# Fewer FFN tiles a pair, scores from a product of the query and key weights, and half-array matmuls in a fused tokenizer, attention and FFN kernel

## The reference

```python
loc  = dwconv(gelu(conv(x, pl_w, stride=16)))          # depthwise 3x3, then 192x192
glob = conv(gelu(dwconv(gelu(conv(wavelet_packet(x), pg_w1)))), pg_w2)
h = (1 - gate) * loc + gate * glob
h = relu(dwconv(h, f1)); h = relu(dwconv(h, f2)); h = dwconv(loc + h, f3)
h = concat([cls, layernorm(h), txt])                    # 1 + 196 + 128 = 325 rows
# attention, each of q, k, v = gelu(x @ w1 + b1) @ w2 + b2 on x = layernorm(h)
scores = (q @ k.T) / SCALE * mask                       # 0 <= i - j < 64, no softmax
h = h + layernorm(scores @ v) * ln_w + ln_b
# FFN: two linear layers, activations rounded to 8 bits a row, weights to -1, 0, 1
h = h + bitlinear(silu(gate) * up, w_out), [up, gate] = bitlinear(layernorm(h), w_in)
```

## Time and profile before

| | us |
|---|---|
| median of the runs | 1199.82 |
| span of the profiled execution | 1195.4 |
| PE busy | 1081.3 (90%) |
| DVE busy | 1033.5 (86%) |
| ACT busy | 963.3 (81%) |
| POOL busy | 812.7 (68%) |

### The profile page before, as it was taken

The page is one execution under the profiler, slowest core; times in us unless marked ns, Lnnn a source line. Parts: engine busy times, 40 slices in busy tenths (PEclk is TensorE's granted clock), DMA queues, the critical chain, the costliest instruction groups (busy, mean ns, idle before and its releaser), DMA issues.

```text
span 1195.4 us, 19559 instructions
## 1 busy us (share of the span) xinstructions
PE 1081.3 (90%) x5674; PEld 736.5 (62%) x5674; DVE 1033.5 (86%) x3013; ACT 963.3 (81%) x2437; POOL 812.7 (68%) x860
## 2 busy tenths in 40 slices
PE   6877999999999999999999999999999897878544
PEld 3655676767676767677676757676766655545311
DVE  1887598999999999999999999999999997856653
ACT  4656687899989898989999988989898978766543
POOL 4446486868687777878686868787786857562521
PEclk9898999999999999999999999999999998979655
DMA  8101010101010100101010101001010000000000
GB/s 327 62 27 41 8 41 7 50 7 57 9 57 9 46 17 16 49 13 50 13 53 7 56 9 54 9 16 50 16 47 15 10 11 15 10 15 9 9 12 14
DMA packets 21513, 40.25 MB, mean 34 GB/s; under 512 B 2656, under 2 KB 18208, under 8 KB 19104
## 3 DMA queue, kind: packets, MB, share of 16 engines
q1 hardware_dynamic: 21408, 39.01, 9.4%
HBM read 31.02 MB, written 7.99 MB: 33 GB/s over the span
## 4 chain that ended last, share of the span: by engine, by line
PE 76%; DVE 9%; ACT 7%; issue 4%; POOL 2%; DMA 1%; SPq 0%; POOLq 0%; DVEq 0%; ACTq 0%
PE bank L398 14%; PE bank L517 7%; PE bank L428 7%; PE bank L439 4%; PE bank L430 4%; PE bank L438 4%; PE bank L376 4%; PE bank L377 3%; PE bank L539 3%; PE bank L458 3%; PE bank L459 3%; DVE bank L1214 2%; PE bank L471 2%; PE bank L472 2%; PE bank L587 2%
## 5 line engine op out<-in xcount | busy, mean ns | idle before, releaser
L1214 DVE SCALAR_TENSOR_TENSOR bank<-padA,c_col,bank 128x406 f32<-128x406 f32 x560 | 357.9, 639 | 7.6
L398 PE MATMUL bank<-x_sb,w_emb 128*128 128x392 f32 x576 | 216.6, 507 | 6.5 <-ACT padA L755 3.7
L810 ACT ACTIVATE prod<-padB,c_col 128x196 f32<-128x196 f32 x432 | 174.3, 449 | 5.1 <-POOL accB L1734 2.5
L1703 POOL TENSOR_TENSOR yg<-y_f,c_gout 128x512 f32<-128x512 f32 (+1 forms) x96 | 122.6, 1278 | 45.9 <-DVE y_f L1404 45.8
L398 PEld LDWEIGHTS bank<-x_sb,w_emb 128*128 128x128 f32 x576 | 102.3, 192 | 60.8 <-ACT padA L755 5.6
L810 ACT ACTIVATE early<-padB,c_col 128x196 f32<-128x196 f32 x288 | 120.7, 449 | 2.3 <-POOL accB L1734 2.2
L517 PE MATMUL bank<-w_in,xq 128*128 128x512 bf16 (+1 forms) x384 | 109.1, 411 | 13.6 <-ACT xq L873 13.6
L1696 POOL TENSOR_TENSOR s<-s,c_mhalf 128x1 f32<-128x1 f32 (+1 forms) x96 | 55.2, 575 | 90.8 <-ACT s L886 90.8
L867 ACT ACTIVATE yq<-bank 128x512 bf16<-128x512 f16 (+1 forms) x96 | 50.2, 523 | 50.8 <-PE bank L529 50.8
L879 ACT ACTIVATE th<-bank,sm 128x512 f32<-128x512 f32 (+1 forms) x96 | 65.3, 681 | 31.6 <-PE bank L517 31.1
L1385 DVE SCALAR_TENSOR_TENSOR ya<-th,bank 128x512 f32<-128x512 f32 (+1 forms) x96 | 65.1, 678 | 26.5 <-ACT th L879 26.3
(11 more groups left out here) (219 smaller groups left out, 3229.3 us busy)
## 6 DMA issues: line engine op xcount, KB each, us to landing
x_sb<-xt SPq DMA_DIRECT2D x16, 1176.0 KB, 5.3
out<-o_sb SPq DMA_DIRECT2D x64, 96.0 KB
w_sq<-squares SPq DMA_DIRECT2D x1, 3840.0 KB, 15.6
h_sb<-txt SPq DMA_DIRECT2D x32, 51.8 KB
out<-o_sb SPq DMA_DIRECT2D x32, 51.8 KB
h_sb<-txt SPq DMA_DIRECT2D x32, 44.2 KB
w_in<-win SPq DMA_DIRECT2D x1, 1024.0 KB, 17.6
c_row<-broads SPq DMA_DIRECT2D x1, 672.0 KB, 19.2
```

The lines of the kernel that those rows point to most:

```text
L398: done = mm(pE[:, 0:2 * N_PATCH], w_emb[:, k, m, :], x_sb[:, k, :], start=k == 0, stop=k == KC - 1)
L810: made = go(grid(prod[ACC[s] ^ 1][:, k, :]), tap_view(padB[min(s, 2)], SIDE, k), ACT.Copy, scale=tapcol(s, 1, k))
L1214: v.scalar_tensor_tensor(grid(acc if k == TAPS - 1 else run), tap_view(pad, ROWS_A, k), tapcol(s, 0, k), grid(run), ALU.mult, ALU.add).the ...
L1703: g.tensor_tensor(yg[0:m, :], y_f[0:m, :], c_gout[0:m, :], ALU.mult).then_inc(f_yg, 1)
```

## The change

Four things are done at once, and the order of every engine's turn is written anew.

1. **Five full FFN tiles a pair.** Rows 256 to 319 of both images make one tile of 128 rows. The last 5 rows of each image are gathered over many pairs in `left`, and worked on as a sixth tile in pairs 11 (120 rows) and 15 (40 rows). There are 82 tiles for 96. `join` on SP copies rows by three transfers inside SBUF: two into `left`, and, after these have landed, one of 64 rows that puts image 1 beside image 0.
2. **Scores from the product of query and key weights.** Once, the kernel computes the product of `qw2` and `kw2` and puts it in the place of `kw2`. The query's second layer and its four evictions on ACT go; scores are taken between the new keys and `hq`. What the query bias contributes for each key row is a vector, nine matmuls of one or two columns a pair, which DVE reads (`key_offsets`) and adds in `scores_out`.
3. **Tiles for half-used matmuls.** The first two matmuls of a square's third chunk become column tiles; the last matmuls of `values` (the two full row tiles), `scores` and `layer_F3` become pairs of row tiles, one for each image.
4. **Order.** All turns are reordered, with 8 stages and 23 turns; PE's first stage with work is now `on[1]`, its last `on[7]`. `values` and `scores` of both images are interleaved.

```diff
             def square(i, chunks, dstA, dstB, n, after):
...
-                mm(dstB, w[:, AB0, :], chunks[0], start=True, stop=False)
-                mm(dstB, w[:, AB1, :], chunks[1], start=False, stop=False)
+                for c in range(2):
+                    mm(dstB[HALF[c]], w[:, AB0 + c, HALF[c]], chunks[c], start=True, stop=False)
                 mm(dstB, w[:, BB, :], chunks[2], start=False, stop=True).then_inc(after, 1)
...
+            def scores(a):
+                took(a, U_K2 + 2)
+                unit_free(a, U_SC)
+                for t in range(TILES):
+                    r = pT[U_SC % 2][0:ROWS[t], R_AT + 2 * t:R_AT + 2 * t + 2]
+                    mm(r, hk[:, 2, tok_cols(t)], c_qk[:, 0:2], start=True, stop=False)
+                    for img in range(2):
+                        mm(r[:, img:img + 1], hk[:, img, tok_cols(t)], c_qk[:, 2:3], start=False, stop=img == 1)
+                unit_free(a, U_SC + 1)
...
-                    mm(dst, k2[:, img, tok_cols(t)], q2[:, img, q], start=True, stop=False)
-                    done = mm(dst, k2[:, 2, tok_cols(t)], q2[:, 2 + img, q], start=False, stop=True)
+                    for img in range(2):
+                        mm(dst[img], k2[:, img, tok_cols(t)], hq[:, img, q], start=True, stop=False)
+                    for img in range(2):
+                        done = mm(dst[img], k2[HALF[img], 2, tok_cols(t)], hq[HALF[img], 2, q], start=False, stop=True)
...
+            def query_key_weights():
+                pe.wait_ge(s_cst, ALL_CONSTS)
...
+                done.then_inc(s_qk, 1)
+                pe.wait_ge(s_qkw, 2)
+                for half in range(2):
+                    for o in range(2):
+                        mm(pT[0][:, half * D:(half + 1) * D], t_k2[cut[o], o, half * P:(half + 1) * P],
+                           t_q2[cut[o], o, 0:D], start=o == 0, stop=o == 1)
...
+            def join(f, par):
+                sp.wait_ge(h2_ready, f + 1)
+                lo = left_rows(f) - 2 * SPARE
+                for img in range(2):
+                    sp.dma_start(left[f > LEFT[0]][lo + img * SPARE:lo + (img + 1) * SPARE, :],
+                                 h2[par][SPAN:ROWS[2], 2 + img * TILES, :]).then_inc(taken, 16)
+                sp.wait_ge(taken, (f + 1) * 32)
+                sp.dma_start(h2[par][SPAN:P, 2, :], h2[par][0:SPAN, 2 + TILES, :]).then_inc(joined, 16)
...
                 for n in tiles:
-                    m = ROWS[n % TILES]
-                    done = v.bn_stats(st_f[0:m, n, :], h2[par][0:m, n, :])
+                    if n == 2:
+                        dve.wait_ge(joined, (f + 1) * 16)
+                    done = v.bn_stats(st_f[:, n, :], h2[par][:, n, :])
...
+            def query_key_blocks():
...
+                dve.wait_ge(s_qk, 1)
+                for t, bank_ in ((t_q2, pT[0]), (t_k2, pT[1])):
...
+                dve.wait_ge(s_qk, 2)
+                w, top, low = w_sq[:, SQUARES.index("kw2")], HALF[0], HALF[1]
+                v.tensor_copy(w[:, AA, :], pT[0][:, 0:P])
...
             def turn(it, par, on):
...
+                if on[5]:
+                    hidden_bn(it - 5, odd, (0, 1, 3))
+                if on[6]:
+                    hidden_round(3, it - 6, 3, par)
+                if on[2]:
+                    taps(it - 2, L_, 6)
+                if on[6]:
+                    hidden_round(4, it - 6, 3, par)
+                    gated(it - 6, 4)
+                if on[2]:
+                    taps(it - 2, L_, 7)
+                if on[6]:
+                    lifted(it - 6, 4)
+                if on[5]:
+                    hidden_bn(it - 5, odd, (4, 2))
```

The last store of a pair with leftover rows is one transfer for each image, 24 for pair 11 and 8 for pair 15:

```diff
+                if n == NF:
+                    for i in range(left_rows(f) // SPARE):
+                        image = 2 * f + 2 - left_rows(f) // SPARE + i
+                        sp.dma_start(out[image, T - SPARE:T, :],
+                                     o_sb[at][i * SPARE:(i + 1) * SPARE, :]).then_inc(stored[at], 16)
```

## The result

The changed kernel takes 1271.24 us (median of 4 runs, 1269.59 to 1274.97) where the one before, beside it, takes 1199.81: a ratio of 1.0604, 95% interval 1.0577 to 1.0631. Slower by 71 us; 1164 was predicted, with a range that ends at 1193.

What follows compares the result with a forecast made beforehand. The prediction took PE to bound the middle of the kernel. From the profiled 1195.4 us, 30 saved in steady turns, 12 saved in the drain and 6 lost in the fill, plus 4.4 to the median, gave 1164 us, range 1132 to 1193.

Steps and rivals of the forecast that it cites:

- its own sign: Stated test: the prediction is wrong if PE rests more than 2 us a turn or the key vector costs over 3.
- PE's sum: PE's work in a middle turn: 3.38 + 1.03 - 1.5 - 0.5 = 2.4 us saved, a turn of 62.5 us.
- the terms 0.01 and 0.04: Tiles on PE: each of five squares gains 0.01 us a turn, each of six row pairs loses 0.04.
- Both stay hidden, and PE is their cover: Middle turns: DVE falls to 60.6 us, 1.9 behind PE, ACT loses work, so neither sets the turn.
- Rival C: The new order leaves holes in PE: 1179 us if half the gain goes, 1194 if all; chance 0.18.
- The steady 30 us: Middle of the kernel: 12.5 turns at 2.4 us each save 30 us (0 to 51).
- so a turn of 62.5 us: Middle: PE's work after the saving of 2.4 us was taken as the length of the turn.
- The fill: Start of the kernel: making the product of the weights in the third turn loses 6 us (0 to 10).
- PE's second step: Fill: PE's multiplication of the query and key weights, after its transposes, put at 3 us.
- The drain: End of the kernel: fewer FFN tiles save 14 us, eight stores cost 2.3, net 12 us saved.
- where the last attention is the limit: Drain: lower bound of 5 us for the tiles' saving, if the last attention limits instead of the FFN tiles.
- Rival D: Slower by the join: two transfer hops of 4.5 us each make DVE wait, 24 us slower, 1224; chance 0.10.

Runs made afterwards that it cites:

- e1: Changed kernel with POOL's sums for layer F3 held back until DVE's `token_scale_3` is through; 1222.8 us, 1.0205 of the kernel before.
- e9: Changed kernel: F3 sums wait, `biased_tokens` later, two EMB_GA chunks earlier, weight product over two turns, SP's stores of tiles 2 and 3 before text loads; 1201.3 us.
- e5: Kernel before with only the column pairs in the five squares and F3's row pairs added; 1201.8 us, 1.0017 of the kernel before.
- e2: Changed kernel with two EMB_GA chunks on PE moved ahead of the pair's first token transposes; 1240.0 us, 1.0341 of the kernel before.
- e16: e9 with the last tile's end earlier on DVE, and on PE one EMB_LA chunk between tile 2's transposes and its `ffn_in`; 1199.7 us, ratio 0.9992.
- e4: Changed kernel with the product of the query and key weights spread over two turns; 1261.0 us, 1.0521 of the kernel before.
- e8: Changed kernel with two POOL gain products cut to one column in the last pair, leaving out most of them; 1266.7 us, ratio 1.0549.

## Why the prediction was wrong

By its own sign, more than 2 us of rest a turn, the prediction was wrong: PE rests 5.7.

*PE's sum: right.* 62.10 to 62.55 us at full clock (e1, e9) for 62.5. The key vector takes 1.63 us (569.09 to 570.72 in the changed kernel) for 1.5; five square and two F3 pairs come to 0.0 a turn (e5), as the terms 0.01 and 0.04 had it. The terms for the values and the scores were not measured by themselves.

*"Both stay hidden, and PE is their cover": the step that failed.* DVE's sum was taken from durations of the kernel before and given as 60.6. It is 58.84 with both collisions removed, and 63.54 as the change stands: 4.7 us a turn from POOL operations that run at the same time, 2.7 of them undone by e1 and 2.0 by moving `biased_tokens`. I had rewritten orders in front of me, looked at POOL's sum only (50 of 65), and did not lay POOL's new list beside DVE's. And DVE's sum was not even what mattered: the stretched steps are a chain that PE waits for. Of the 6.8 us between 69.3 and 62.5, 3.1 are that wait, 1.3 the clock behind it, and 2.4 the small waits. The first two are shown by e1 and e2.

*Rival C, holes in PE, was the right kind* with 18 in 100, but it was priced as a loss of the gain, 1194 at most. Nothing in it let a hole cost more than the change had saved, or let the clock add to it. Its size is what failed: holes of 5.7 us a turn for a saving of 2.

*The steady 30 us: the second step that failed, "so a turn of 62.5 us".* The small waits stay when the collisions are gone: e16, the fastest of the runs that leave nothing out, has PE rest some 2 us a turn and equals the kernel before. That 62.5 us of PE's work makes a turn of 62.5 was assumed from an order that left 0.4 us of rest. With one tile less there is less to put between the steps of a tile; that this is the reason was only argued. What order would give the 2 us back stays open.

*The fill: 17 us for 6.* The terms were taken at 4 us for DVE's copies and 3 for PE's second step. PE's second step, and DVE's wait for it:

```profile
48.40 3.82 PE L705 MATMUL bank<-y_f,r 128*128 128x192 f32 x8 [2.76 <-DVE r L1578]
52.15 2.12 PE L710 MATMUL bank<-c_col,r 128*128 128x1 f32 x8
54.20 2.12 PE L710 MATMUL bank<-c_col,y_f 128*128 128x1 f32 x8
56.25 1.10 PE L713 MATMUL bank<-c_qk,c_ones 128*128 128x1 f32 x4
```

```profile
57.39 0.29 DVE L1582 COPY w_sq<-bank 128x128 f32<-128x128 f32 x1 [9.04 <-PE bank L713]
```

PE's second step took 8.9 us, behind a rest of 2.76, with a granted clock of 0.50 all through, the lower of its two levels, 1.2 of 2.4 GHz, and PE's next layer stood behind it. DVE's fifteen copies, the other term, last 0.15 to 0.42 us each, 4.0 in sum, as assumed. Spreading the product brought back 10 us (e4).

*The drain: 5.0 us lost for 12 gained.* The bracket "where the last attention is the limit" was there, at 5 us gained; it is what happens. Pair 14's tiles are done, and then PE waits 8.4 us for the first tile of pair 15:

```profile
1213.60 0.40 PE L601 MATMUL bank<-c_id,r 128*128 128x128 f16 x2 [8.38 <-ACT r L971]
```

Its attention ends later after the last `mix` than before: the output's gain starts 152.4 us behind it, 145.8 before. The tokens' gain, ahead of the attention, already starts 4.9 of these 6.6 us later (77.8 us; 72.9 before), and behind the attention 3.2 us are won back. That this is what delays the attention is not shown, as the 1.6 us that e8 takes out there are lost on the way. e8 shows the limit; why the attention comes later was not tried.

*Rival D.* `joined` is absent among DVE's waits in the middle, as expected; in the drain DVE waits 0.8 us for it. D was the only rival with a slower kernel, and it is not what happened.

## What to carry to other kernels

When an order is rewritten, lay VectorE's chains of small SBUF steps beside GpSimd's new list, not only the engines' sums: here a step of 0.17 us that met a GpSimd operation lasted until that was through. Look at the longest of a short step in the trace before, not only at its mean or median: one turn there showed 2.49 us for 0.26. A sum over the bounding engine is a floor; before it is called a forecast, ask for each rest what the engine has to do in it. And follow an operation that is moved through every queue that waits for it: here POOL to SP to a store to DVE.

## What was not expected of the hardware

Six-column steps of DVE lasted 0.41 to 2.52 us instead of 0.15 to 0.23 under POOL's operations, and ended 0.02 to 0.03 us behind them. In the kernel before, 0.2 us of order between the two engines made 0.26 us or 2.49 of the same step. There the gain of the FFN's tokens (`w_g`, two inputs in SBUF) has a mean of 0.58 us from 300 to 1000 us, where the changed kernel shows 0.41; that this is the same effect was not tried. A rest of 3.05 us on PE cost another 1.3 us by a granted clock of 0.59 behind it; behind 1.6 us of rest in e2 the clock of the turn was 1.00. Seven matmul pairs on half arrays, of 192 and 196 columns, changed a turn of 64.9 us by 0.0.
